# Another order at the seams of a transformer iteration: output projection in single PSUM banks ahead of the FFN, down projections in halves

## The reference

```python
x = L0_attn_a_x
x = x + _L0_attn_a_ref(_layernorm(x, axis=-1), L0_attn_a_W_qkv, L0_attn_a_b_qkv, L0_attn_a_W_out, L0_attn_a_b_out)
x = x + _L0_ffn_ref(_layernorm(x, axis=-1), L0_ffn_w_gate, L0_ffn_w_up, L0_ffn_w_down)
x = x + _L0_attn_b_ref(_layernorm(x, axis=-1), L0_attn_b_w_qkv, L0_attn_b_b_qkv, L0_attn_b_w_proj, L0_attn_b_b_proj)
x = x + _L0_ffn_ref(_layernorm(x, axis=-1), L0_ffn_w_gate, L0_ffn_w_up, L0_ffn_w_down)
```

## Time and profile before

| | |
|---|---|
| median of 3 runs | 2245.91 us (2243.66 to 2246.78) |
| profiled execution, its span | 2243.9 us |
| PE busy | 2137.2 us, 95% of the span |
| DVE, POOL, ACT busy | 1269.9, 668.7, 531.7 us |
| HBM traffic | 36 GB/s over the span |

### The profile page before, as it was taken

One profiled execution on the slowest core, in us unless ns is written; L12 is line 12 of the kernel. 1 busy time (PEld: TensorE's weight loads), 2 busy tenths in 40 slices (PEclk: granted clock), 3 DMA queues, 4 the chain that ended last, 5 costly groups with the idle time before them and its releaser, 6 DMA issues.

```text
span 2243.9 us, 34194 instructions
## 1 busy us (share of the span) xinstructions
PE 2137.2 (95%) x11056; PEld 1502.9 (67%) x11056; DVE 1269.9 (57%) x2475; ACT 531.7 (24%) x1076; POOL 668.7 (30%) x508
## 2 busy tenths in 40 slices
PE   6999989999999999999989999999999999999998
PEld 5555478888755447888765554788886554578886
DVE  6767464545576646445447665544555666454444
ACT  1344410000144441000104454100011444310001
POOL 3323223332312322323231233232323223233332
PEclk9999999999999989999999999999999999999998
DMA  4332101111323211111142321111113232011112
GB/s 129 89 86 67 30 29 57 48 57 38 77 68 77 67 39 38 48 48 47 66 124 68 77 67 39 38 52 43 47 39 77 68 89 63 29 47 47 57 38 94
DMA packets 59745, 135.10 MB, mean 60 GB/s; under 512 B 10784, under 2 KB 11808, under 8 KB 59552
## 3 DMA queue, kind: packets, MB, share of 16 engines
q1 hardware_dynamic: 59552, 132.71, 20.9%
HBM read 77.62 MB, written 4.19 MB: 36 GB/s over the span
## 4 chain that ended last, share of the span: by engine, by line
PE 84%; issue 7%; DVE 4%; POOL 2%; ACT 1%; DMA 1%; SPq 1%; DVEq 0%; POOLq 0%; ACTq 0%
PE ring L872 13%; PE ring L873 13%; PE ring L874 13%; PE bank L982 12%; PE ring L936 8%; PE bank L960 7%; PE bank L872 6%; PE bank L873 6%; PE bank L874 6%; PE ring L863 1%; DVE attn L645 1%; POOL area L426 1%; DVE xn L682 1%; ACT prob L543 1%; DVE xn L645 1%
## 5 line engine op out<-in xcount | busy, mean ns | idle before, releaser
L872 PE MATMUL ring<-xt_hi,area 128*128 128x512 f32 x1248 | 492.0, 394 | 11.2 <-DVE xt_lo L654 8.1
L873 PE MATMUL ring<-xt_lo,area 128*128 128x512 f32 x1248 | 488.3, 391 | 0.0
L874 PE MATMUL ring<-xt_hi,area 128*128 128x512 f32 x1248 | 488.1, 391 | 0.0
L682 DVE CUSTOM_DVE_ANT_0 xn<-ring,mask_row 128x128 bf16<-128x128 f32 (+7 forms) x512 | 374.9, 750 | 131.4 <-PE ring L936 126.6
L543 ACT ACTIVATE prob<-bank 128x512 f32<-128x512 f32 (+3 forms) x768 | 335.4, 489 | 345.0 <-PE bank L960 344.0
L424 POOL TENSOR_SCALAR area<-w_stage 128x1024 fp32r<-128x1024 f32 x131 | 145.5, 1111 | 820.2 <-PE bank L874 432.5
L743 DVE TENSOR_TENSOR prob<-prob,ring 128x512 f32<-128x512 f32 x128 | 88.0, 687 | 450.2 <-ACT prob L561 450.1
L426 POOL TENSOR_TENSOR area<-w_stage,area 128x1024 fp32r<-128x1024 f32 x131 | 322.6, 2462 | 10.9
L561 ACT ACTIVATE prob<-ring 128x512 f32<-128x512 f32 x128 | 76.6, 598 | 999.5 <-PE ring L874 999.5
L872 PEld LDWEIGHTS ring<-xt_hi,area 128*128 128x128 f32 x1248 | 235.5, 189 | 71.3 <-issue 9.8
L874 PEld LDWEIGHTS ring<-xt_hi,area 128*128 128x128 f32 x1248 | 235.4, 189 | 49.8
(11 more groups left out here) (76 smaller groups left out, 2088.0 us busy)
## 6 DMA issues: line engine op xcount, KB each, us to landing
w_stage<-ffn_w SPq DMA_DIRECT2D x96, 512.0 KB, 3.3
area<-kq_parts SPq DMA_DIRECT2D x336, 128.0 KB, 2.3
w_stage<-attn_w SPq DMA_DIRECT2D x35, 512.0 KB, 3.3
x<-x_in SPq DMA_DIRECT2D x24, 256.0 KB, 3.7
area<-attn SPq DMA_DIRECT2D x48, 128.0 KB, 2.3
out<-x SPq DMA_DIRECT2D x16, 256.0 KB, 2.1
bias_rows<-row_bias SPq DMA_DIRECT2D x10, 256.0 KB, 4.1
area<-nm_hi SPq DMA_DIRECT2D x32, 8.0 KB, 1.8
```

Source lines behind the costliest of these rows:

```text
L682: dve.tensor_tensor_reduce(out=sum_out[:, RING[name] % 2, 0:keys], in0=src[:, 0:keys], in1=mask_row[:, TOKENS - keys:], scale=1.0, scalar= ...
L872: pe.matmul(dst, ah, bh, start=first and k == 0, stop=False)
L873: pe.matmul(dst, ah, bl, start=False, stop=False)
L874: ins = pe.matmul(dst, al, bh, start=False, stop=last and k == n - 1)
```

## The change

- The output projection of the second chunk (`op` 4 to 7) goes to the four single banks and runs straight after attention, three of its four head groups for all tiles first (`BUT_LAST`), then the last one; both gate/up tiles of step 0 follow it. ACT copies unit 7's result ahead of its table load. DVE adds the projection before `hidden_parts(0, 0)`.
- `down(0)` and `down(15)` are cut in halves, one for each hidden tile of 128; a transpose pair lies before each half of `down(0)`, and both pairs of `ln1` between the halves of `down(15)`. DVE makes step 15's first hidden parts ahead of the statistics of the next iteration.
- Two value tiles instead of four go through the ring, and six through the single banks; the fourth is made after the q projection. DVE takes value tile 0 ahead of the second chunk's statistics.
- `transpose_max` of units 1, 3 and 5 (`MAX_LATE`) runs after the first quarter of the next projection instead of at the end of the unit before. In unit 6 the `s1` tiles, the reciprocals and `mt` are spaced otherwise, in unit 7 `op` and `ln2` run earlier and at other points, and ACT copies unit 5's result after four exponentials instead of after two.
- POOL splits units 5 and 6 before a weight slot instead of after it, and waits for all of the second layer norm's `xn` before it splits the third weight slot and those behind it of an FFN.

```diff
-EARLY = {1: 2, 3: 12, 5: 12, 7: 14}
+EARLY = {1: 2, 3: 12, 5: 12, 7: 12}
...
     if u == UNITS - 1:
-        return [9, 11, 13, 15, 23, 27]
+        return [6, 8, 10, 12, 21, 25]
+    if u == UNITS - 2:
+        return [0, 2, 4, 6, 10]
...
+        def value_bank(t):
+
+            return bank[(t - RING_VALUES) % CT][:, :]
...
                 for u in range(UNITS):
+                    if u == UNITS - 1:
+                        for w in range(UNITS - 3, UNITS - 1):
+                            split_attn(it, w)
                     if u in SPLIT_BEFORE:
                         split_weights(it, SPLIT_BEFORE[u])
...
                 split_weights(it, FFN_SLOT0 + 2)
                 inverse_deviation(it, 1, 1)
 
+                wait_alone(pool, xn_ready, it * 2 * TT + 2 * TT)
                 for i in range(FFN_SLOT0 + 3, SLOTS + 2):
                     split_weights(it, i)
...
-                        exps(u, 0, range(0, 2))
+                        exps(u, 0, range(GH))
                         if u < UNITS - 1:
                             evacuate(u - 1)
-                        exps(u, 0, range(2, GH))
...
+                evacuate(UNITS - 1)
                 load_table(ACT.Silu)
-                evacuate(UNITS - 1)
...
-                chunk_stats(it, 1, b + 1)
                 dve.wait_ge(bias_loaded, it * 48 + 48)
                 take_v(0)
+                chunk_stats(it, 1, b + 1)
+                take_v(1)
                 normalise_pair(it, 0, 2)
                 normalise_pair(it, 0, 3)
-                for t in range(1, CT):
-                    take_v(t)
+                take_v(2)
                 qk_to_lo(0, 0)
+                take_v(3)
...
+                        elif u == UNITS - 2:
+                            some_recips(2)
...
-                hidden_parts(0, 0)
                 for t in range(CT, TT):
                     add_projected(t)
                 chunk_variance(it, 1, 1)
                 normalise_pair(it, 1, 2)
                 normalise_pair(it, 1, 3)
+                hidden_parts(0, 0)
                 hidden_parts(0, 1)
...
+                hidden_parts(STEPS - 1, 0)
                 chunk_stats(it + 1, 0, b + layer + 1)
                 normalise_pair(it + 1, 0, 0)
                 normalise_pair(it + 1, 0, 1)
-                hidden_parts(STEPS - 1, 0)
                 hidden_parts(STEPS - 1, 1)
...
-                        pe.wait_ge(ring_drained, buffer_free(it, name))
+                        if t < CT:
+                            pe.wait_ge(ring_drained, buffer_free(it, name))
+                        elif t >= CT + 2:
+                            pe.wait_ge(evacuated, it * UNITS + UNITS)
...
                         project(u + 2, 0, 0)
+                        if u in MAX_LATE:
+                            transpose_max(u)
                         weigh_last()
...
+                for groups in (BUT_LAST, LAST_GROUP):
+                    for t in range(CT, TT):
+                        project_out(t, groups)
                 gate_up(0, 0)
-                for groups in (BUT_LAST, LAST_GROUP):
-                    for t in (CT, CT + 1):
-                        project_out(t, groups)
-                for t in range(CT + 2, TT):
-                    project_out(t)
                 gate_up(0, 1)
-                transpose_pair(it, 1, 2)
-                transpose_pair(it, 1, 3)
-                down(0)
+                for t in range(BT):
+                    transpose_pair(it, 1, 2 + t)
+                    down(0, range(t, t + 1))
...
+                down(STEPS - 1, range(1))
                 transpose_pair(it + 1, 0, 0)
                 transpose_pair(it + 1, 0, 1)
-                down(STEPS - 1)
+                down(STEPS - 1, range(1, BT))
```

More of the change, by code:

```diff
@@ L124, in ring_order @@
 def ring_order():
-    yield from (("ln1", 0), ("ln1", 1), *(("v", t) for t in range(CT)))
+    yield from (("ln1", 0), ("ln1", 1), *(("v", t) for t in range(RING_VALUES)))
     yield from (("q", 0), ("ln1", 2), ("k", 0), ("ln1", 3), ("q", 1), ("k", 1))
@@ L131, in ring_order @@
         yield from beside(u)
-    yield ("gu", 0, 0)
-    yield from (("op", t) for t in range(CT, TT))
-    yield from (("gu", 0, 1), ("ln2", 2), ("ln2", 3))
+    yield from (("gu", 0, 0), ("gu", 0, 1), ("ln2", 2), ("ln2", 3))
     yield from (("gu", s, t) for s in range(1, STEPS) for t in range(BT))
@@ L256, in block_kernel, with rows_taken @@
         RING_CREDIT = 2
+        ROWS_CREDIT = CT
+        def rows_taken(it, row):
+            return it * ROWS + row + 1 + ROWS_CREDIT
         def parts_of(u):
@@ L1040, in project_whole @@
                         project(u, w, half)
+                for t in range(CT - 1):
+                    value_tile(t)
                 project_whole(0, 0)
+                value_tile(CT - 1)
                 transpose_pair(it, 0, 2)
```

81 lines of the change are left out of this document (49 added, 32 removed).

## The result

The changed kernel takes 2177.32 us (median of 4 runs, 2176.04 to 2179.44) against 2246.35 of the kernel before in the same comparison (4 runs, 2243.66 to 2251.65): a ratio of 0.9696, 95% interval 0.968 to 0.9712, 69 us less. The profiled execution has a span of 2177.7 us against 2243.9, 66.2 less.

What follows compares the result with a forecast made beforehand. PE was taken as the bound, busy 2137.2 of 2243.9 us, with waits that also lower its clock. Terms -41.3 - 7.4 - 10.5 - 3 - 3.6 - 2 + 3.8 = -64.0 gave span 2179.9, median 2182 us, range 2165 to 2202.

Steps and rivals of the forecast that it cites:

- FFN start: Four stretches from attention's end to `gate_up(1, 0)`: reordered work hides DVE's chain and keeps the full clock, 41.3 us less.
- The strict rule for POOL's port: At the FFN starts, both hidden parts would queue behind POOL's whole instructions on the port shared with DVE; 3 us a start.
- Layer seams: Last gate/up product to k projection: value wait and wait ahead of k go, 22.9 against 26.64 us, twice: 7.4 us less.
- 22.1 + 0.8 = 22.9: Layer seam length in us: 22.1 of PE work plus waits of 0.5 for the ring and 0.3 for a hidden part.
- Batch seam: Value 0 no longer waits for the DMA, and the next batch's `x` lands earlier; k projection starts sooner, 10.5 us less.
- End and start: At the launch's end DVE adds the last rows 3.7 us earlier, stores and loads queue: 3 us less; no start term.
- Attention: Unit 6 saves 3.6 us, unit 7 saves 2, later `mt` of units 1, 3 and 5 costs 3.8.
- (a): Clock stays low at the FFN start because of attention's thin last steps, not the wait: 2190 us, chance 0.10.
- (d): Waits only move: the chain beside PE at the FFN start is some 12 us longer; 2240 to 2250, chance 0.03.
- (c): Row maxima of units 1, 3 and 5 queue behind the next unit's twelve stacking DMAs on SP: 2260, chance 0.04.
- (b): POOL's splits hold up both hidden parts whole: 3 us an FFN start instead of 0.7; 2191, chance 0.10.
- (e): More is hidden: no cost for `mt` and POOL, and the small waits all go: 2168 us, chance 0.11.

Runs made afterwards that it cites:

- e6: The changed kernel with ACT's table load again ahead of its copy of unit 7: 2178.96 us.
- e5: The changed kernel with the output projections and transposes of unit 7 at their old points: 2177.74 us.
- e2: The changed kernel with down(15) whole behind both transpose pairs and DVE's step 15 hidden parts behind the normalisation: 2179.1 us.
- i4: The changed kernel with the next iteration's statistics ahead of step 15's first hidden part on DVE: 2177.31 us.
- e7: The changed kernel with ACT's copy of unit 5 back after two exponentials of unit 6: 2187.16 us.
- i2: The changed kernel with unit 7's transposes earlier and six output projection matmuls ahead of the last weighing: 2174.22 us.
- e1: The changed kernel with the row-max transposes of units 1, 3 and 5 back at the end of the unit before: 2176.17 us.
- i5: The changed kernel with the edits of i4, i2 and e1 together: 2171.39 us.

## Why the prediction was right, step by step

It came out 4.7 us above the median: the span was forecast at -64.0 us and is at -66.2. The two largest terms came out where they were put; attention came out larger by luck, and the layer seams smaller.

**FFN start**: -41.3 forecast, -42.2 measured. The chain beside PE ran as worked out: `xn` ready at 18.2 (18.6), transposes at 21.85 (21.8), second pair at 25.9 (25.5), end at 29.7 (29.9 with the 0.7 for POOL). Two of its steps were off without a cost. The strict rule for POOL's port held: the first hidden part is 2.8 us longer, more than the 2.41 that were called the worst, and the second 2.2. The 2.3 and 2.0 us that the prediction called spare were used up whole, and a little more: the parts end at 302.73 and 306.70, PE starts on them at 302.95 and 306.76, and some 0.5 us a start are lost where 0.7 was taken. And ACT's copy was given credit for "over a us" and for a split that would else be "just late": e6 shows 0.7 us and a split that is in time without it, at 7.3, since the earlier marks help too (e5).

**Layer seams**: -7.4 forecast, -5.0 measured, the one term that was plainly too large. The step that failed is "22.1 + 0.8 = 22.9": it counted PE's work and DVE's waits, and not that the instruction queue must get through the end of the loop while 12 matmuls, 3 us, are all that is queued behind the last wait. The seams came out at 23.89 and 24.39, with 1.13 and 1.62 us of "issue"; the 0.35 us for the ring and 0.3 for the second hidden part are the forecast 0.8. e2 and i4 take the "issue" away in two ways and reach 22.2 to 23.1. That it is the jump of the loop itself is argued from its place; that it is a delay covered by queued matmuls is shown.

**Batch seam**: -10.5 forecast, -10.9 measured. DVE sees the landing 2.8 us earlier against the last gate/up product (1.8 to 3.7 forecast) and the k projection starts 7.5 us behind it (7.7). Part of it was clock: 0.82 before, 1.00 after. The wait for `xn` is 1.36 us where 2 to 4 were expected, and 1.08 for q's split stands behind it. No run puts value tile 0 back behind the statistics, so that this order brings the gain is read from the two traces, by the 7.13 us wait that is gone, and not tested by itself.

**End and start**: -3 forecast, -2.5 measured at the end; 0.9 us less at the start of the launch were not forecast, and are less than the 2 us by which that start differs between the runs.

**Attention**: -1.8 forecast, -4.7 measured, but not for its reasons. Iteration 1 of before has a stretch at the lower level of 1.2 GHz behind the wait of unit 6, which the prediction had in its trace and did not count. Windows of the kernel before:

```profile
780.00:785.00 5.00, 3.98 (x14) 1.28 (x13) 1.10 (x2) 2.64 (x6) 0.64 (x1) 0.66 0.00 2
...
785.00:790.00 5.00, 5.00 (x23) 2.01 (x22) 0.89 (x1) 1.53 (x4) 0.64 (x1) 0.50 0.00 0
...
790.00:795.00 5.00, 5.00 (x31) 1.85 (x23) 1.82 (x7) 1.15 (x4) 0.64 (x1) 0.50 0.01 2
...
795.00:800.00 5.00, 5.00 (x35) 3.12 (x34) 4.97 (x8) 0.49 (x2) 4.04 (x3) 0.64 0.36 111
```

and the same stretch of time in the changed kernel, which has come to the start of unit 7 there (at its unit 6, 765 to 770 us, the clock is 1.00):

```profile
780.00:785.00 5.00, 4.34 (x17) 1.44 (x15) 3.66 (x9) 3.26 (x6) 1.06 (x2) 0.86 0.20 75
...
785.00:790.00 5.00, 5.00 (x27) 1.68 (x24) 0.00 (x0) 2.24 (x5) 4.21 (x3) 0.80 0.00 0
```

The first costs 6.6 us (248.33 against 241.7), the falls of the changed kernel in iterations 1 and 2 about 1.5 each. That leaves 3.6 of the 4.7 us to the clock, and this is luck: no term counted it. Without the falls an attention takes 241.7 before (242.42 in iteration 3) and 241.5 to 241.6 after, 1.1 us less over the launch where 1.8 was forecast. The terms: at unit 6, 0.9 us an iteration was forecast and e7 shows 0.7. At unit 7 0.5 was forecast, and the earlier marks bring nothing (e5): the idle time for exponentials fell (in iteration 0 from 2.41 to 0.93 us for units 6 and 7 together), but that for POOL's masks at the diagonal, which was not forecast, rose from 0.5 to 1.8. These waits stood behind the ones that were removed; i2 shows them worth 1.1 us an iteration. For `mt` late, +0.95 was forecast and e1 shows +0.8, but not by the step that was worked out: `nm_lo` costs 0.66 us an iteration and not 2.7, the rest came at the `s1` tiles. That the sum agrees is luck as well.

**Rivals**: (a) and (d) fall with the windows at 29.7 us and a clock of 1.00, (c) with waits of at most 0.5 us for the row maxima. Of (b) the mechanism was true and the price was not: the hidden parts were held up for 2.8 and 2.2 us, and PE lost 0.5 and not 3 a start. (e) fails with the small waits, which did not go, and with e1, by which the late `mt` costs what was taken.

## What to carry to other kernels

Work the engine that bounds out against the chain beside it from event to event, and the moved order's stretch comes out to a few tenths; the time at a lower clock behind a wait belongs to the price of that wait (behind the 2.03 us at the first start the granted clock was 0.57 for 4 us). Where two engines share a port, move the one with slack beside work that has slack too: here the same POOL instructions cost PE 2.6 us more beside one DVE step than beside another. At a loop's end, count the matmuls that are queued behind the last wait that holds PE up, and look for the wait that stands second before crediting the first.

## What the runs showed of the hardware

- The end of an iteration needs cover on TensorE's queue. In the changed kernel and the seven runs with its seam, 4.2 to 4.9 us pass from the end of the last hidden part, for which PE waits, to the first matmul of the next iteration (554.13 to 558.35 at the first seam), with 3.05 us of matmuls to hide it, and 1.1 to 1.8 us are idle. With 24 matmuls behind the last wait (e2) there is no gap at the layer seams, and with 12 but the wait over earlier (i5) at most 0.4 us, which is a wait for DVE. What in the loop's end takes the time is not shown.
- In attention the clock falls behind small waits in a row of small matmuls, and not each time. In the profiled runs made from the changed kernel the falls inside attention lie at the start of unit 6, behind waits of 0.27 and 0.40 us (0.97 in e7), or of unit 7, behind 0.45 and 0.21 us, apart from some that come behind the waits of the batch seam and reach into the attention of iteration 2. The same waits stand in each iteration, yet two of four show a fall in the changed kernel and none in e5. A short fall costs 1.5 us, the long one of the kernel before 6.6, and two in one attention 3 to 4 (i5, e7). That is the size by which the runs of one kernel differ, and the granted clock of a run goes with its time: in e7 from 0.996 at 2183.14 us to 0.993 at 2190.50.
